# Splitting six PSUM banks four and two between maxima and scores in a 16-head attention

## Chip, cores and metric

One Trainium2 chip, one of its cores. The metric is the device time of one execution in microseconds (us). The kernel before takes 4480.93 us (median of three runs, 4480.48 to 4482.56).

## The reference

Eight sequences of 512 rows and 256 columns go through four layers. Each layer adds an attention and a feed-forward part to `x`. The change lies in the first three attention-like parts, which all have 16 heads of 16 columns: the cross attention of layer 0, the mixture-of-heads attention that is layer 0's feed-forward part, and the cross attention of layer 1. Cut to what matters:

```python
q, k, v = heads(xn @ Wq + bq), heads(ctx @ Wk + bk), heads(ctx @ Wv + bv)   # 16 heads of 16
a = softmax(q @ k.T / sqrt(16))            # 512 x 512 for each head
x = x + merge(a @ v) @ Wo + bo
```

In the mixture part `q` is normalised by head and scaled, and the heads' sum is weighted by gates.

## The kernel before, in words

`softmax_attentions` does the three parts in one phase of 24 rounds: 3 parts by 8 sequences. The phase's exponentials run from 77.3 to 1747.7 us of the trace. A round is written as 32 steps (`STEPS`), and each engine walks the same steps by itself, tied to the others only by semaphores. There is no planner: the order is the tables `TURNS` (line 120) and the step functions.

For every head two products are made of the same operands. The first product, keys on the free axis, is there for its row maximum alone: TensorE writes a 128 x 512 tile `ps_max` (`for_maximum`, line 753), VectorE reduces it to one number for each row (`maximum`, line 482, the instruction at 485). The maxima, negated and split in two, are turned round on TensorE (`negmax` fill, line 827) and copied by ScalarE into eight extra rows of the query stack (`take_negmax`, line 684), so that the second product, keys on partitions, comes out with the maximum taken off: `ps_sc` (`score`, line 738). ScalarE takes its exponential to `probs` (`exponentials`, line 664, the instruction at 671). Every fourth step TensorE multiplies the last eight tiles of `probs` by the values (`values`, line 763, instruction at 774), into `ps_out`. The maxima run 12 steps (`LEAD`) ahead of the scores.

A step on TensorE is: the fills that are due (projections, turns, `negmax`, `raw`, `y`; all go to the one bank `ps_t` and each waits for the previous one to have been taken out), score, maximum, score, maximum, and after every step with remainder 1 of 4 a group of values. In the step behind the values the order is maximum, score, score, maximum (line 865). A round has 64 scores, 64 maxima and 8 groups of values.

PSUM has eight banks of 128 x 512 numbers: three for `ps_max`, three for `ps_sc`, one each for `ps_out` and `ps_t`. Score number `at` goes to bank `at % 3` and waits for exponential `at - 3`; a maximum's product waits in the same way for reduction `at - 3`. TensorE carries out its instructions in the order written, so a wait of either kind holds back all behind it.

VectorE also takes `v`, `raw` (lines 511 and 513), `y` (line 590 in a cross round, 594 in a mixture round) and `gates`, normalises rows, and does the mixture's small gate work (lines 561 to 579). ScalarE also copies `ps_out` after steps 2, 10, 18 and 26 (`take_out`, line 679), and takes `k`, `q`, `xnT`, `hT` (lines 693 to 701) and `negmax`. The rest of the program, five further phases from about 1750 us on, is left alone.

Of the kernel before, what the change touches and what calls it, by code (L numbers as in the profile page):

```python
# [16 lines left out]
F32 = mybir.dt.float32  # L17
# [3 lines left out]
ACT = mybir.ActivationFunctionType  # L21
AX = mybir.AxisListType

P = 128
SEQS = 8
S = 512
# [122 lines left out]
def softmax_attentions(nc, T, G, name, kind):  # L149
# [9 lines left out]
    q_part, k_part = part_terms()  # L159
    ROWS = HD * len(q_part)  # L160
    LEAD = 12
    BANKS = 3
    SLOTS = 6
    PER = 4
    x_sb, ident, identb, own_rows = G["x"], G["ident"], G["identb"], G["own"]
    with Phase(nc, name) as ph:
# [21 lines left out]
        qstack = [ph.sb(f"qstack{b}", [ROWS + 8, HEADS, S], BF16) for b in range(2)]  # L188
        kstack = [ph.sb(f"kstack{b}", [ROWS + 8, HEADS, S], BF16) for b in range(2)]
        vpad = [ph.sb(f"vpad{b}", [P, TILES, HEADS * (HD + 1) + 15], F32) for b in range(2)]  # L190
        maxes = ph.sb("maxes", [P, TILES, HEADS], F32)
        negmax = ph.sb("negmax", [P, 2, TILES, 4, 2], BF16)
        probs = ph.sb("probs", [P, SLOTS, 2, S], F32)
# [23 lines left out]
        gpart = ph.sb("gpart", [P, TILES], F32)  # L217
        ffo = ph.sb("ffo", [P, 2, D], F32)

        ps_max = ph.ps("ps_max", [P, BANKS, S], F32)  # L220
        ps_sc = ph.ps("ps_sc", [P, BANKS, S], F32)
        ps_out = ph.ps("ps_out", [P, S], F32)
        ps_t = ph.ps("ps_t", [P, S], F32)

# [9 lines left out]
        max_ps, max_taken, neg_step, negmax_ready = (ph.sem("max_ps"), ph.sem("max_taken"), ph.sem("neg_step"),  # L234
                                                     ph.sem("negmax_ready"))
        score_ps, probs_ready, probs_used, out_taken = (ph.sem("score_ps"), ph.sem("probs_ready"),
                                                        ph.sem("probs_used"), ph.sem("out_taken"))
# [199 lines left out]
        def _(dve):  # L437
            V = nc.vector
# [43 lines left out]
            def maximum(q, unit):  # L482
                head, t = unit // 4, unit % 4
                dve.wait_ge(max_ps, q.count(64, unit + 1))
                V.tensor_reduce(maxes[:, t, head:head + 1], ps_max[:, q.count(64, unit) % BANKS, :], AX.X,  # L485
                                ALU.max).then_inc(max_taken, 1)

            def negated(q, g):
# [110 lines left out]
            def steps(q):  # L599
# [3 lines left out]
                for n in range(STEPS):  # L603
# [16 lines left out]
                    if own.there:  # L620
                        maximum(own, 2 * (m % STEPS))
                        maximum(own, 2 * (m % STEPS) + 1)
                        if m % 8 == 7:
                            negated(own, (m % STEPS) // 8)
# [28 lines left out]
        def _(act):  # L653
# [10 lines left out]
            def exponentials(q, n):  # L664
                step = q.count(STEPS, n)
                if step >= SLOTS and (step - SLOTS) % PER == 0:
                    act.wait_ge(probs_used, (step - SLOTS) // PER + 1)
                for j in range(2):
                    at = q.count(64, 2 * n + j)
                    act.wait_ge(score_ps, at + 1)  # L670
                    nc.scalar.activation(probs[:, step % SLOTS, j], ps_sc[:, at % BANKS, :], ACT.Exp,  # L671
                                         scale=HD ** -0.5).then_inc(probs_ready, 1)

            def take_out(q, g):
# [61 lines left out]
        def _(pe):  # L736
            weights_here(pe, Item(0))
            def score(q, n, j):

                g, kt, pair = n // 8, n % 8 // 2, n % 2  # L740
                if n % 8 == 0 and j == 0:
                    pe.wait_ge(taken["negmax"], q.count(4, g + 1))
                if not q.later and n == 0 and j == 0:
                    pe.wait_ge(even_own_ready, 1)
                    pe.wait_ge(odd_own_ready, 1)
                at = q.count(64, 2 * n + j)
                if at >= BANKS:
                    pe.wait_ge(probs_ready, at - BANKS + 1)
                head = 4 * g + 2 * pair + j
                nc.tensor.matmul(ps_sc[:, at % BANKS, :], kstack[q.parity][:, head, kt * P:(kt + 1) * P],  # L750
                                 qstack[q.parity][:, head, :], start=True, stop=True).then_inc(score_ps, 1)

            def for_maximum(q, unit):
                head, t = unit // 4, unit % 4
                if unit == 0:
                    pe.wait_ge(stack_in, q.count(192, 192))
                at = q.count(64, unit)
                if at >= BANKS:
                    pe.wait_ge(max_taken, at - BANKS + 1)
                nc.tensor.matmul(ps_max[:, at % BANKS, :], qstack[q.parity][0:ROWS, head, t * P:(t + 1) * P],  # L760
                                 kstack[q.parity][0:ROWS, head, :], start=True, stop=True).then_inc(max_ps, 1)

            def values(q, first, waited):
# [2218 lines left out]
def more_scratch(nc, T):  # L2982
# [4 lines left out]

PHASES = [
    (softmax_attentions, "L0x", ""),
    (quantised_ffn, "L1f", ""),  # L2990
    (feature_attention, "L2x", ""),
# [66 lines left out]
```

## Time and profile before

| | |
|---|---|
| Median of three runs | 4480.93 us |
| The profiled execution: its time, and its span from first to last instruction | 4479.25 us, 4477.1 us |
| TensorE, VectorE, ScalarE, GpSimd busy over the span | 94%, 66%, 57%, 18% |
| The phase, 77.3 to 1747.7 us | 24 rounds |
| A cross round between cross rounds | 68.2 us |
| A mixture round between mixture rounds | 75.3 us |
| The last two rounds | 60.0 and 54.3 us |

Times in the profile are microseconds unless marked ns. TensorE has two rows: PE is the matmuls, PEld the loading of weights, which runs while an earlier matmul is under way. "Idle before" is an engine's idle time just ahead of an instruction, with what ended it. L485 is line 485.

### The profile page before, as it was taken

What the parts mean: (1) busy time and instruction counts of PE and PEld (TensorE: products, weight loads), DVE (VectorE), ACT (ScalarE), POOL (GpSimd) and SP (SyncE); (2) the same over time, 40 slices, a digit from 0 to 9 for tenths busy, and PEclk for the clock granted to TensorE, in tenths of its full rate; (3) what the DMA queues carried; (4) which work ended last, traced back from release to release, by engine and by line L of the source; (5) the groups of instructions that cost most, each with busy time, mean ns of one, the idle gap of its engine ahead of it and who ended that gap; (6) DMA issues with size and microseconds to landing.
All of it is one profiled execution on the core that took longest, in us unless ns stands there. A gap on an engine that the chain in (4) does not pass through costs nothing. (4 is left out here: it accounts for less than half of the span.)

```text
span 4477.1 us, 66439 instructions
## 1 busy us (share of the span) xinstructions
PE 4224.6 (94%) x23716; PEld 2400.0 (54%) x23750; DVE 2965.5 (66%) x7431; ACT 2542.5 (57%) x6408; POOL 811.8 (18%) x576
## 2 busy tenths in 40 slices
PE   6999999999999997888989999999999998999999
PEld 2343344444343342577446666666666665556555
DVE  5767777777777675967765677676676766334333
ACT  3767666666666765743546676767777675111111
POOL 2322444443322311622000000000000000000000
PEclk9999999999999998999999999999999999999999
DMA  8456455445455461000100100110101102000000
GB/s 160 74 78 85 65 66 80 60 64 68 68 75 83 66 83 61 1 20 10 76 12 27 37 30 28 32 32 27 32 27 32 33 26 73 5 5 5 10 5 10
DMA packets 182844, 204.97 MB, mean 46 GB/s; under 512 B 44651, under 2 KB 165099, under 8 KB 180854
## 3 DMA queue, kind: packets, MB, share of 16 engines
q1 hardware_dynamic: 180886, 199.15, 24.3%
q8 instruction: 192, 3.15, 0.3%
q10 hardware_dynamic: 1632, 1.57, 0.3%
q14 instruction: 134, 1.10, 0.1%
HBM read 139.90 MB, written 60.78 MB: 45 GB/s over the span
## 5 line engine op out<-in xcount | busy, mean ns | idle before, releaser
L485 DVE TENSOR_REDUCE L0x_maxes<-L0x_ps_max 128x1 f32<-128x512 f32 x1536 | 976.2, 683 | 288.6 <-PE L0x_ps_max L760 287.0
L671 ACT ACTIVATE L0x_probs<-L0x_ps_sc 128x512 f32<-128x512 f32 x1536 | 822.6, 607 | 360.7 <-PE L0x_ps_sc L750 356.7
L760 PE MATMUL L0x_ps_max<-L0x_kstack,L0x_qstack 96*128 96x512 bf16 x1536 | 587.3, 383 | 22.6 <-DVE L0x_maxes L485 21.3
L2765 ACT ACTIVATE L3x_pexp<-L3x_ps,L3x_nmax 128x77 f32<-128x77 f32 (+2 forms) x1536 | 601.4, 433 | 0.0
L750 PE MATMUL L0x_ps_sc<-L0x_qstack,L0x_kstack 104*128 104x512 bf16 x1536 | 557.0, 383 | 11.5 <-ACT L0x_probs L671 11.0
L2647 DVE TENSOR_REDUCE L3x_nmax<-L3x_ps 128x2 f32<-128x154 f32 (+2 forms) x768 | 346.3, 506 | 242.5 <-PE L3x_ps L2878 240.1
L2773 ACT COPY L3x_pT<-L3x_ps 128x512 f32<-128x512 f32 x512 | 275.1, 593 | 225.8 <-PE L3x_ps L2886 225.4
L2265 ACT ACTIVATE L3f_act_g<-L3f_ps_gu 128x512 f32<-128x512 f32 x128 | 76.4, 597 | 542.4 <-PE L3f_ps_gu L2311 542.3
L774 PE MATMUL L0x_ps_out<-L0x_probs,L0x_vpad 128*32 128x512 f32 x3072 | 369.4, 598 | 1.1 <-ACT L0x_probs L671 1.1
L2663 DVE TENSOR_SCALAR L3x_pexp<-L3x_pexp,L3x_rsum 128x77 f32<-128x77 f32 (+2 forms) x1536 | 357.7, 305 | 6.8
L2765 ACT ACTIVATION_READ_ACCUMULATOR L3x_pexp<-L3x_ps,L3x_nmax 128x1 f32 x1536 | 359.6, 235 | 0.0
L2208 DVE TENSOR_TENSOR L3f_h<-L3f_act_g,L3f_ps_gu 128x512 f32<-128x512 f32 x128 | 88.0, 687 | 383.4 <-ACT L3f_act_g L2265 383.1
L760 PEld LDWEIGHTS L0x_ps_max<-L0x_kstack,L0x_qstack 96*128 96x128 bf16 x1536 | 150.8, 98 | 282.7 <-DVE L0x_maxes L485 168.0
L2904 PE MATMUL L3x_ps<-L3x_pT,L3x_v 128*64 128x128 f32 x4096 | 279.9, 279 | 0.7 <-ACT L3x_oT L2781 0.7
L2886 PEld LDWEIGHTS L3x_ps<-ident,L3x_pexp 128*128 128x128 f32 x2048 | 239.1, 141 | 73.4 <-issue 55.5
L2886 PE MATMUL L3x_ps<-ident,L3x_pexp 128*128 128x128 f32 x2048 | 266.1, 273 | 0.9 <-DVE L3x_pexp L2663 0.9
L750 PEld LDWEIGHTS L0x_ps_sc<-L0x_qstack,L0x_kstack 104*128 104x128 bf16 x1536 | 150.4, 98 | 211.2 <-ACT L0x_probs L671 81.1
L2608 POOL TENSOR_TENSOR L3x_v<-L3x_v,L3x_relv 128x256 f32<-128x256 f32 x32 | 23.4, 731 | 1294.1 <-ACT L3x_v L2748 1294.1
L2311 PE MATMUL L3f_ps_gu<-L3f_xnT,L3f_wg 128*128 128x512 f32 x512 | 243.1, 597 | 1.8 <-DMA L3f_wd<-in_L3f_wd 1.8
L2322 PE MATMUL L3f_ps_y<-L3f_wd,L3f_h 128*128 128x256 f32 x1024 | 242.4, 380 | 1.5 <-DVE x_res L2218 1.5
L2904 PEld LDWEIGHTS L3x_ps<-L3x_pT,L3x_v 128*64 128x64 f32 x4096 | 218.3, 136 | 43.4 <-issue 42.5
L2311 PE MATMUL L3f_ps_gu<-L3f_xnT,L3f_wu 128*128 128x512 f32 x512 | 241.0, 593 | 0.0
(377 smaller groups left out, 6823.5 us busy)
## 6 DMA issues: line engine op xcount, KB each, us to landing
L0x_kstack<-parts_scratch SPq DMA_DIRECT2D x141, 256.0 KB, 10.0
L0x_qstack<-parts_scratch SPq DMA_DIRECT2D x141, 256.0 KB, 14.5
parts_scratch<-L0x_kparts SPq DMA_DIRECT2D x24, 768.0 KB, 3.7
parts_scratch<-L0x_qparts SPq DMA_DIRECT2D x24, 768.0 KB, 5.0
rel_scratch<-L3x_rel_e SPq DMA_DIRECT2D x32, 408.0 KB, 2.4
L3x_rel_d<-prob_scratch SPq DMA_DIRECT2D x32, 408.0 KB, 3.1
L0x_kv_in<-in_ctxT SPq DMA_DIRECT2D x16, 512.0 KB, 4.2
L3x_rel_t<-rel_scratch SPq DMA_DIRECT2D x32, 154.0 KB, 2.3
```

What stands on the lines that cost most here:

```text
L485: V.tensor_reduce(maxes[:, t, head:head + 1], ps_max[:, q.count(64, unit) % BANKS, :], AX.X, ALU.max).then_inc(max_taken, 1)
L671: nc.scalar.activation(probs[:, step % SLOTS, j], ps_sc[:, at % BANKS, :], ACT.Exp, scale=HD ** -0.5).then_inc(probs_ready, 1)
L750: nc.tensor.matmul(ps_sc[:, at % BANKS, :], kstack[q.parity][:, head, kt * P:(kt + 1) * P], qstack[q.parity][:, head, :], start=True, stop ...
L760: nc.tensor.matmul(ps_max[:, at % BANKS, :], qstack[q.parity][0:ROWS, head, t * P:(t + 1) * P], kstack[q.parity][0:ROWS, head, :], start=T ...
L774: i = nc.tensor.matmul(ps_out[32 * j:32 * j + 32, :], vpad[q.parity][:, kt, (HD + 1) * head:(HD + 1) * head + 32], probs[:, q.count(STEPS, ...
L2311: i = nc.tensor.matmul(ps_gu[:, n % 2, k], w[:, ci, n * P:(n + 1) * P], xnT[:, ci, :], start=(ci == 0), stop=(ci == C - 1))
L2647: i = V.tensor_reduce(nmax[:, n % 4, s], ps[:, bank:bank + 2, a:b], AX.X, ALU.max, negate=True)
L2663: i = V.tensor_scalar(pexp[:, m % 4, e, a:b], pexp[:, m % 4, e, a:b], rsum[:, m % 4, s, e:e + 1], None, ALU.mult)
L2765: i = nc.scalar.activation(pexp[:, n % 4, e, a:b], ps[:, SB + 2 * (n % 2) + e, a:b], ACT.Exp, bias=nmax[:, n % 4, s, e:e + 1], accum_out=s ...
L2773: nc.scalar.copy(pT[:, m % 2, e], ps[:, TB + e]).then_inc(pt_ready, 1)
L2886: i = nc.tensor.transpose(ps[:, TB + e, kt * P:(kt + 1) * P], pexp[:, m % 4, e, kt * P:(kt + 1) * P], ident[:])
L2904: i = nc.tensor.matmul(ps[DIMH * e:DIMH * (e + 1), OB, at:at + P], v[g % 2][:, vt, h * DIMH:(h + 1) * DIMH], pT[:, m % 2, e, kt * P:(kt + ...
```

## The change

The one constant `BANKS = 3` becomes two: the maxima get four banks, the scores two. The allocations, the bank numbers and the distances of the two waits follow.

```diff
-    BANKS = 3
+    MAX_BANKS = 4
+    SCORE_BANKS = 2
...
-        ps_max = ph.ps("ps_max", [P, BANKS, S], F32)
-        ps_sc = ph.ps("ps_sc", [P, BANKS, S], F32)
+        ps_max = ph.ps("ps_max", [P, MAX_BANKS, S], F32)
+        ps_sc = ph.ps("ps_sc", [P, SCORE_BANKS, S], F32)
...
-                V.tensor_reduce(maxes[:, t, head:head + 1], ps_max[:, q.count(64, unit) % BANKS, :], AX.X,
+                V.tensor_reduce(maxes[:, t, head:head + 1], ps_max[:, q.count(64, unit) % MAX_BANKS, :], AX.X,
...
-                    nc.scalar.activation(probs[:, step % SLOTS, j], ps_sc[:, at % BANKS, :], ACT.Exp,
+                    nc.scalar.activation(probs[:, step % SLOTS, j], ps_sc[:, at % SCORE_BANKS, :], ACT.Exp,
...
-                if at >= BANKS:
-                    pe.wait_ge(probs_ready, at - BANKS + 1)
+                if at >= SCORE_BANKS:
+                    pe.wait_ge(probs_ready, at - SCORE_BANKS + 1)
...
-                nc.tensor.matmul(ps_sc[:, at % BANKS, :], kstack[q.parity][:, head, kt * P:(kt + 1) * P],
+                nc.tensor.matmul(ps_sc[:, at % SCORE_BANKS, :], kstack[q.parity][:, head, kt * P:(kt + 1) * P],
...
-                if at >= BANKS:
-                    pe.wait_ge(max_taken, at - BANKS + 1)
-                nc.tensor.matmul(ps_max[:, at % BANKS, :], qstack[q.parity][0:ROWS, head, t * P:(t + 1) * P],
+                if at >= MAX_BANKS:
+                    pe.wait_ge(max_taken, at - MAX_BANKS + 1)
+                nc.tensor.matmul(ps_max[:, at % MAX_BANKS, :], qstack[q.parity][0:ROWS, head, t * P:(t + 1) * P],
```

## Rows read from the trace of the kernel before

**Rows 1.** The page, busy time (share of the span) and instructions

```profile
PE 4224.6 (94%) x23716; PEld 2400.0 (54%) x23750; DVE 2965.5 (66%) x7431; ACT 2542.5 (57%) x6408; POOL 811.8 (18%) x576
```

**Rows 2.** Stretches: length; busy of PE, PEld, DVE, ACT, POOL; PEclk; DMA; GB/s

```profile
345.20:413.40 68.20, 66.17 (x354) 27.08 (x352) 48.98 (x98) 47.28 (x82) 19.71 (x12) 1.00 0.54 78
...
1000.40:1075.70 75.30, 70.25 (x386) 32.36 (x384) 58.05 (x122) 47.57 (x82) 34.11 (x15) 0.98 0.47 63
```

**Rows 3.** Waits of PEld in the phase: total us, times, longest

```profile
PEld L0x_ps_max L760 <- DVE L0x_maxes L485: 159.3, 230, 2.8
PEld L0x_ps_sc L750 <- ACT L0x_probs L671: 81.1, 185, 0.9
```

**Rows 4.** The same in one cross round, 413.4 to 481.6 us

```profile
PEld L0x_ps_max L760 <- DVE L0x_maxes L485: 6.0, 9, 0.8
PEld L0x_ps_sc L750 <- ACT L0x_probs L671: 3.4, 8, 0.9
```

**Rows 5.** Timeline of PEld in that round: start, us, [idle before, releaser]

```profile
413.69 0.10 PEld L760 LDWEIGHTS L0x_ps_max<-L0x_kstack,L0x_qstack 96*128 96x128 bf16 x1 [0.53 <-DVE L0x_maxes L485]
...
417.06 0.10 PEld L760 LDWEIGHTS L0x_ps_max<-L0x_kstack,L0x_qstack 96*128 96x128 bf16 x1 [0.84 <-DVE L0x_maxes L485]
...
439.62 0.10 PEld L760 LDWEIGHTS L0x_ps_max<-L0x_kstack,L0x_qstack 96*128 96x128 bf16 x1 [0.51 <-DVE L0x_maxes L485]
...
441.79 0.42 PEld L782 LDWEIGHTS L0x_ps_t<-ident,L0x_xn 128*128 128x128 f32 x4 [0.84 <-ACT L0x_qstack L684]
```

**Rows 6.** Timeline of the last round, where no maxima are left

```profile
1733.60 5.01 ACT L671 ACTIVATE L0x_probs<-L0x_ps_sc 128x512 f32<-128x512 f32 x10
...
1739.36 0.33 PEld L750 LDWEIGHTS L0x_ps_sc<-L0x_qstack,L0x_kstack 104*128 104x128 bf16 x3 [0.84 <-ACT L0x_probs L671]
...
1739.85 1.09 ACT L671 ACTIVATE L0x_probs<-L0x_ps_sc 128x512 f32<-128x512 f32 x2 [1.25 <-PE L0x_ps_sc L750]
1740.50 0.10 PEld L750 LDWEIGHTS L0x_ps_sc<-L0x_qstack,L0x_kstack 104*128 104x128 bf16 x1 [0.81 <-ACT L0x_probs L671]
```

**Rows 7.** The page's group of the exponentials: busy, mean ns of one, idle before

```profile
L671 ACT ACTIVATE L0x_probs<-L0x_ps_sc 128x512 f32<-128x512 f32 x1536 | 822.6, 607 | 360.7 <-PE L0x_ps_sc L750 356.7
```

**Rows 8.** Timeline of the cross round behind 413 us, places that are priced

```profile
417.77 1.08 ACT L671 ACTIVATE L0x_probs<-L0x_ps_sc 128x512 f32<-128x512 f32 x2 [2.24 <-PE L0x_ps_sc L750]
...
417.95 0.38 PE L750 MATMUL L0x_ps_sc<-L0x_qstack,L0x_kstack 104*128 104x512 bf16 x1
...
421.13 0.20 PEld L827 LDWEIGHTS L0x_ps_t<-identb,L0x_negmax 128*8 128x8 bf16 x4 [0.65 <-DVE L0x_htok L513]
...
458.92 1.08 ACT L671 ACTIVATE L0x_probs<-L0x_ps_sc 128x512 f32<-128x512 f32 x2
...
459.87 0.38 PE L750 MATMUL L0x_ps_sc<-L0x_qstack,L0x_kstack 104*128 104x512 bf16 x1
...
467.31 2.05 ACT L671 ACTIVATE L0x_probs<-L0x_ps_sc 128x512 f32<-128x512 f32 x4
...
467.95 0.39 PE L750 MATMUL L0x_ps_sc<-L0x_qstack,L0x_kstack 104*128 104x512 bf16 x1
...
474.37 2.10 ACT L671 ACTIVATE L0x_probs<-L0x_ps_sc 128x512 f32<-128x512 f32 x4
```

**Rows 9.** Timeline of a mixture round at its second `y` fill

```profile
1052.44 1.59 PEld L795 LDWEIGHTS L0x_ps_t<-L0x_wo_mixture,L0x_hT 128*128 128x128 f32 x8 [0.84 <-ACT L0x_qstack L684]
...
1057.04 0.88 DVE L594 SCALAR_TENSOR_TENSOR L0x_ffo<-L0x_ps_t,L0x_gscale,L0x_bo_mixture 128x256 f32<-128x256 f32 x2
...
1058.56 0.10 PEld L760 LDWEIGHTS L0x_ps_max<-L0x_kstack,L0x_qstack 96*128 96x128 bf16 x1 [2.84 <-DVE L0x_maxes L485]
1058.57 2.65 PEld L795 LDWEIGHTS L0x_ps_t<-L0x_wo_mixture,L0x_hT 128*128 128x128 f32 x8
```

**Rows 10.** Stretches there, columns as in rows 2: idle ahead, then that fill

```profile
1055.90:1058.40 2.50, 0.12 (x1) 0.00 (x0) 2.43 (x5) 1.14 (x3) 1.29 (x2) 1.00 0.25 90
1058.50:1061.30 2.80, 2.73 (x8) 2.21 (x9) 1.80 (x4) 0.00 (x0) 2.72 (x3) 0.64 0.54 188
```

## The prediction

> **What bounds the kernel now.** I read the page's busy line first: TensorE is busy 94% of the span, VectorE 66%, ScalarE 57% [rows 1]. Then the stretches cut at the rounds of the phase that the change touches. In a cross round of 68.2 us TensorE is busy 66.17, VectorE 48.98 and ScalarE 47.28 us, and a mixture round of 75.3 us looks alike with 70.25, 58.05 and 47.57 [rows 2]. So TensorE bounds the phase. The other two have room on average, and what they can do is make TensorE wait for a bank. Any such wait that nothing later absorbs is added to the time, because TensorE works through its instructions in order.
>
> Third, the list of waits of the weight loads. In the phase they waited for a reduction 230 times, 159.3 us in all, and for an exponential 185 times, 81.1 us [rows 3]. Read plainly, the maxima wait twice as long, and a fourth bank is for them. The timeline says otherwise. The load behind each group of values shows 0.84 us idle whatever comes there: 0.84 put down to the reduction at 417.06, and 0.84 put down to a copy of ScalarE ahead of a turn at 441.79 [rows 5]. That is the tail of the values' own matmuls, not a bank. In the cross round behind 413.4 us nine waits for a reduction make 6.0 us [rows 4]. Four of them are such tails; five are real, 6.0 less 3.36, or 2.64 us: three in a row before the values at 415.2, of which 413.69 is the first, one before a projection, and that of 0.51 at 439.62 [rows 5]. A load of 0.10 us that follows the last one at 0.22 has 0.12 ahead of it anyway, so the five are worth about 2.05 us of a round. The score side has eight, 3.4 us [rows 4].
>
> **The fourth bank of the maxima.** No instruction is added or taken. The reductions stay as many, 64 a round, and VectorE stays in order. At most the 2.05 us of a cross round go. Not all will: a product that no longer waits for its own bank soon meets a fill, which waits for VectorE or ScalarE to have taken the last one out of the only `ps_t`, or a score.
>
> **The bank that the scores lose.** A score now waits for the exponential two before it. Three numbers decide. Alone, from the score's load to its exponential's start is 0.49 us (1739.36 to 1739.85, [rows 6]); the exponential takes about 0.60 (mean 607 ns, [rows 7]); the next load follows its end by 0.05 (1740.50, [rows 6]). So a bank comes round in 1.14 us, and two banks allow a score every 0.57. ScalarE with a full queue does ten in 5.01, one every 0.50 [rows 6]. TensorE itself can issue a score and a product in 0.44, at 0.22 each. So whenever TensorE has just come from values or a fill, and could run ahead by a third score, it stops. Because a load runs 0.21 us ahead of its matmul, about the first 0.15 us of lateness costs nothing.
>
> I carried this through one cross round, from one group of values to the next, with the durations of the trace. Where a delay meets a fill that waits for VectorE or ScalarE anyway, it vanishes; where it comes right before values, it stays. What stays, in order:
> - Step 3, score matmul at 417.95. Its exponential two before starts at 417.77 and ends 0.6 later, so the score goes at 418.43, 0.48 late. The product of a maximum behind it is late with it, VectorE's reductions end 0.32 later, and the `negmax` fill, which waits for VectorE at 421.13, is 0.32 late [rows 8]: +0.32.
> - The eight steps behind: +0.07, since the fourth bank gives most back at the `v` fill.
> - Before the values at 441: the 0.51 wait at 439.62 goes [rows 5] and a score wait of half its worth comes: -0.17.
> - Before the values at 460: the matmul of 459.87 must wait for the second of the pair that starts at 458.92 and lasts 1.08 [rows 8]: 460.00 and 0.07 make 460.07: +0.20.
> - Behind these values: +0.16.
> - Before the values at 468.5: four exponentials from 467.31 in 2.05 us, late because ScalarE takes `q` first. The score at 467.95 waited for the first; with two banks it waits for the second, one exponential later [rows 8]: +0.49. The whole of a lost bank, right ahead of the values.
> - Steps 27 to 29: four from 474.37 in 2.10, behind the copy of `ps_out` [rows 8]. The third score comes 0.98 late, the maxima with it, the `negmax` fill again waits for the reductions: +0.30.
> - Behind the last values: +0.25 by the next `raw` fill.
> - Steps 0 and 1: the three waits that begin with that of 0.53 [rows 5] go, and scores at the loop's 0.57 take their place: -0.05.
> That is +1.57, and about 0.1 more because I took the loop 0.05 too short in two places: +1.7 us for a cross round. ScalarE's whole list for these rounds stays as long as it was.
>
> A mixture round keeps less. Its fills are longer and absorb more, the same walk leaves +0.24, +0.49, +0.22, +0.29 and +0.20 with -0.05: +1.4. And it holds the one long wait on a reduction, 2.84 us before 1058.56, behind the gates' small operations [rows 9]. With a fourth bank the product goes before them. The second `y` fill then waits only for VectorE's taking of the first, done at 1057.04 plus 0.88, or 1057.92 [rows 9], where the bank came free only with the reduction behind it. That is some 0.6 us, and as the fill's place is then set by VectorE, 0.4 of the delay before it is absorbed. The clock adds to it: after 2.50 us with TensorE busy for 0.12, the granted clock is 0.64 of full over the next 2.8 us [rows 10], so part of it at the 1.2 GHz level, and this fill takes 2.65 us where the first took 1.59 [rows 9]. With products and scores moved into the gap it shrinks to about 1.3 us, and I take the clock to stay: 0.8 of the 1.06 us reach the path. So 1.4 less 1.8: -0.4. Such rounds are five.
>
> **The sum.** Ten plain cross rounds at +1.7: +17. Six rounds at the borders of the parts, which mix the fills of both kinds, at +1.0, between the two: +6. Five mixture rounds: -2. The first round, +2. The last two have few fills between scores. In the last no maxima are left, TensorE stands between loops of exponentials, and three of its eight groups of values come one exponential (0.49) later, with 20 scores at 0.57 in place of 0.50: +3.5, and +2.5 for the one before it. In all +29 us. The phases behind are shifted, not changed. Against the profiled execution, 4479.25 us: 4508. The median of the runs is 1.7 above it, so 4510 by that; I say 4509.
>
> Bounds: from below, all 2.05 us of a cross round's waits on reductions come back and no score costs anything, -49 us over 24 rounds. From above, each of the 192 stretches between values keeps one whole exponential of 0.49 and the maxima give nothing: +94. My sum stands between, since I found a full 0.49 in one of the eight stretches.
>
> **Rivals.** *Faster: the reductions' waits were the dearer ones.* The place is the step before values and before a fill; the price is half to all of the 49 us, 4432 to 4456. It decides if the score's wait stays below the 0.15 us that the early load hides. The Trainium skill ("Perfetto Trace Analysis", Optimization Strategy) has it that the same gap repeating on the engine that should be saturated can mean that PSUM has too few buffers. The gaps repeat here, but the larger part is the values' tail [rows 4, 5], and there are as many real gaps on the side that loses a bank. Chance 0.07.
>
> *No change.* Two banks are enough for an engine that is busy 47.28 of 68.2 us [rows 2], and every delay falls where a fill waits anyway. For it: five of my nine places have a small sum. Against it: two are right ahead of values, where nothing absorbs. 4472 to 4488, chance 0.10.
>
> *Much slower.* Delays pile up over several stretches, or the clock falls more often. One fall costs about the 1.06 us of that fill and as much in what is behind it; once a round it is some 40 us more, 4550. In cross rounds the granted clock is 1.00 [rows 2] with eight score waits, none near 2.5 us. The Trainium skill ("TensorE: Matmul & The Clock Gate", A second HAM failure mode) warns of bank cycling that lets TensorE idle in short pieces until the clock oscillates; the trace does not show it at these lengths. Chance 0.09.
>
> That the change does not do what it says I leave out: eight banks are used before and after, and 64 tiles a round divide by four and by two.
>
> **The numbers.** The forecast, 4490 to 4536, has 0.74; over 4536 0.09; within 0.2% of before (9 us, about what can be told from no change) 0.10; faster 0.07. So slower 0.83. The range is 4486 to 4536.
>
> **What would show it.** In the changed profile: waits on line 750 for line 671 well over 185, and over 81 us; the 0.5 us waits before 413 and 439 gone, the 0.84 ones still there; cross rounds near 69.9 us, mixture rounds near 75 with no fall of the clock, the last near 58; line 485 and line 671 unchanged in busy time. I am wrong if cross rounds are at or below 68.2, or if mixture rounds keep the fall.

## The result, and the profile after

The changed kernel takes 4507.39 us (median of four runs, 4504.70 to 4509.49) against 4480.70 for the kernel before beside it: a ratio of 1.006, 95% interval 1.0048 to 1.0073. It is 27 us slower; the forecast was 4509.

The profiled execution took 4505.59 us, its span is 4503.7, so 26.6 above the span before. That is three things. The phase, from the first to the last exponential group, runs from 71.9 to 1774.7 us, 1702.8 against 1670.4 before: +32.4. It began 5.4 us earlier. What lies behind it takes 2729.0 against 2729.4.

The earlier start has two parts. From the first product for a maximum to the first exponential it is 14.2 us (57.7 to 71.9) where it was 16.4 (60.9 to 77.3). Most of that part belongs to the change: over all profiles of this study the same stretch takes 14.2 to 15.2 us in the five kernels with four banks for the maxima, 16.0 to 17.2 in the seven with three, and 20.0 with two. The forecast had no term for it. The other 3.2 us lie ahead of that first product, whose place varies from 57.6 to 60.9 us between profiles; nothing explains that here. So the length of the phase and of single rounds are the finer measures, and both are used below.

The page's busy line and the stretches (columns as in [rows 2]) of the changed kernel. The four stretches are a cross round, a mixture round, a border round and the last round; then the whole phase.

```profile
PE 4232.0 (94%) x23750; PEld 2361.7 (52%) x23750; DVE 2974.4 (66%) x7431; ACT 2558.2 (57%) x6408; POOL 812.4 (18%) x576
...
346.50:416.30 69.80, 66.76 (x354) 25.95 (x354) 49.34 (x99) 47.96 (x81) 19.71 (x12) 1.00 0.52 76
1008.10:1083.50 75.40, 69.87 (x386) 30.00 (x386) 59.01 (x123) 47.92 (x82) 34.14 (x15) 1.00 0.48 63
631.50:706.70 75.20, 69.62 (x370) 28.35 (x370) 54.00 (x102) 47.78 (x81) 31.62 (x13) 0.98 0.48 64
1717.40:1774.70 57.30, 51.02 (x284) 17.28 (x282) 30.93 (x58) 42.66 (x73) 0.00 (x0) 1.00 0.00 1
71.90:1774.70 1702.80, 1602.08 (x8567) 637.37 (x8567) 1230.15 (x2469) 1143.81 (x1916) 553.84 (x277) 1.00 0.49 69
```

Nothing of the work has changed: the shares of the page are those of [rows 1], and a cross round has VectorE busy for 49.34 us (48.98 before) and ScalarE for 47.96 (47.28). The round is 1.6 us longer all the same (69.8 against 68.2). The time is in waits. Those of the weight loads, in the phase (total us, times, longest) and then in the cross round behind 416.3 us, which answer to [rows 3, 4]:

```profile
PEld L0x_ps_sc L751 <- ACT L0x_probs L672: 276.6, 639, 1.2
PEld L0x_ps_max L761 <- DVE L0x_maxes L486: 65.4, 78, 0.8
...
PEld L0x_ps_sc L751 <- ACT L0x_probs L672: 11.7, 27, 0.9
PEld L0x_ps_max L761 <- DVE L0x_maxes L486: 2.5, 3, 0.8
```

The waits on a reduction fell from 230 to 78. Those 78 are all the values' tail, 0.84 us each, 65.4 in all: no real wait for a bank of the maxima is left. In the kernel before 95 of the 230 were such tails and 135, of 79.7 us together, were real. The waits on an exponential rose from 185 to 639 and from 81.1 to 276.6 us. In the cross round they are 8.3 us more and the round is 1.6 us longer; the real waits on reductions that went make 2.6 of the difference, and the rest lies where TensorE would have waited anyway. The timeline of the weight loads shows two places of that round:

```profile
419.80 0.10 PEld L761 LDWEIGHTS L0x_ps_max<-L0x_kstack,L0x_qstack 96*128 96x128 bf16 x1 [0.84 <-DVE L0x_maxes L486]
...
421.16 0.10 PEld L751 LDWEIGHTS L0x_ps_sc<-L0x_qstack,L0x_kstack 104*128 104x128 bf16 x1 [0.81 <-ACT L0x_probs L672]
...
421.64 0.10 PEld L751 LDWEIGHTS L0x_ps_sc<-L0x_qstack,L0x_kstack 104*128 104x128 bf16 x1 [0.37 <-ACT L0x_probs L672]
...
424.20 0.20 PEld L828 LDWEIGHTS L0x_ps_t<-identb,L0x_negmax 128*8 128x8 bf16 x4 [0.97 <-DVE L0x_htok L514]
...
471.30 0.10 PEld L751 LDWEIGHTS L0x_ps_sc<-L0x_qstack,L0x_kstack 104*128 104x128 bf16 x1 [0.89 <-ACT L0x_probs L672]
...
471.78 0.10 PEld L751 LDWEIGHTS L0x_ps_sc<-L0x_qstack,L0x_kstack 104*128 104x128 bf16 x1 [0.37 <-ACT L0x_probs L672]
...
472.32 0.16 PEld L775 LDWEIGHTS L0x_ps_out<-L0x_probs,L0x_vpad 128*32 128x32 f32 x8 [0.43 <-issue]
```

The first line is the tail of values, the same 0.84 us as in [rows 5], put down to a reduction by chance. The next three lines are the forecast's step 3: scores held at 421.16 and 421.64, the maxima's products behind them late, and the `negmax` fill still waiting for VectorE, with 0.97 us idle ahead where 0.65 stood [rows 8]. The last three are the place with a whole exponential right ahead of values.

Both kernels issue the same loads in the same order, so they can be laid side by side from the first values of the round. By how much more the changed kernel is late at each place, in us:

| Place in the cross round | Measured | Forecast |
|---|---|---|
| Step 3, up to the `negmax` fill | +0.33 | +0.32 |
| The eight steps behind | +0.09 | +0.07 |
| Before the values at 441 | -0.17 | -0.17 |
| Before the values at 460 | +0.20 | +0.20 |
| Behind these values | +0.17 | +0.16 |
| Before the values at 468.5 | +0.49 | +0.49 |
| Steps 27 to 29 | +0.41 | +0.30 |
| Behind the last values, with steps 0 and 1 | +0.05 | +0.20 |
| The round | +1.57 | +1.57, 1.7 with the allowance |

And all rounds, from first exponential to first exponential:

| Rounds | Measured | Forecast |
|---|---|---|
| The first | +2.1 | +2 |
| Ten cross rounds (+1.55 to +1.63 each) | +15.7 | +17 |
| Six border rounds (+0.2, +0.3, +4.0, +0.5, +2.8, +3.1) | +10.9 | +6 |
| Five mixture rounds (-0.2, -1.3, and +0.0 to +0.1 three times) | -1.3 | -2 |
| The last two | +2.1 and +2.9 | +2.5 and +3.5 |
| The phase | +32.4 | +29 |

The -1.3 of one mixture round is a fall of the granted clock in the kernel before that lasted 6.8 us there (from 830.6) and 3.4 in the four others: that round took 76.6 us, those 75.3 to 75.5. And the first round's +2.1 stands against the 2.2 us gained ahead of it: from the first product for a maximum to the round's end it is 79.6 us against 79.7 (80.4 in a second profile of the changed kernel, number 11).

In a mixture round the forecast's long wait is gone and the clock stays up (columns of the timeline as above):

```profile
1060.88 1.59 PEld L796 LDWEIGHTS L0x_ps_t<-L0x_wo_mixture,L0x_hT 128*128 128x128 f32 x8 [0.84 <-ACT L0x_qstack L685]
...
1066.17 1.59 PEld L796 LDWEIGHTS L0x_ps_t<-L0x_wo_mixture,L0x_hT 128*128 128x128 f32 x8 [1.52 <-DVE L0x_ffo L595]
```

The second `y` fill waits for VectorE's taking of the first, 1.52 us where a product stood for 2.84 (TensorE is idle for 1.02 and 2.55 of them, by the matmuls), and takes 1.59 where it took 2.65 [rows 9]; from fill to fill it is 5.29 against 6.13. The stretch with this fill gains 2.1 us. Yet the round is 75.4 us, not shorter than before. What took it back stands at its end, in two rows of VectorE and GpSimd:

```profile
1075.67 1.27 POOL L394 TENSOR_TENSOR x_res<-x_res,L0x_ffo 128x512 f32<-128x512 f32 x1
1075.99 0.99 DVE L493 TENSOR_SCALAR L0x_negmax<-L0x_maxes 128x16 bf16<-128x16 f32 x1
```

The negation of 16 numbers a row, 0.18 us when it runs alone, takes 0.99 and ends 0.04 us behind GpSimd's addition of the output. The `negmax` fill waits for it. The round is shifted enough for these two to meet, as they do in all five mixture rounds: steps 27 to 29 cost +1.1 us where +0.29 was forecast. The border round at 631.5 us has the same thing with a split of the queries:

```profile
696.44 0.18 DVE L493 TENSOR_SCALAR L0x_negmax<-L0x_maxes 128x16 bf16<-128x16 f32 x1
696.64 2.12 POOL L381 TENSOR_TENSOR L0x_qparts<-L0x_qf,L0x_qparts 128x1024 bf16<-128x1024 f32 x1
696.65 2.15 DVE L495 SCALAR_TENSOR_TENSOR L0x_negmax<-L0x_maxes,L0x_negmax 128x16 bf16<-128x16 f32 x1
698.91 0.23 PEld L828 LDWEIGHTS L0x_ps_t<-identb,L0x_negmax 128*8 128x8 bf16 x4 [2.38 <-issue]
```

The weight loads stand for 2.38 us, and the granted clock falls to the 1.2 GHz level for 3.4 us from 700 us on. (In the kernel before the negation was held there too, for 1.26 us at 690.1, and the loads stood for 1.66. In the first two border rounds it went the other way: the negation took 0.89 and 0.90 us at 548.0 and 619.3 before, and is not held with the change, so those rounds grow by 0.2 and 0.3 only.) The changed kernel has such falls at 700, 1195 and 1270 us, the kernel before had one in each mixture round, near 755, 831, 909, 984 and 1059. The falls at 1195 and 1270 follow no long wait: over the 45 us ahead of each, TensorE is busy for 42.86, and no load waited longer than 1.3 us.

### The profile page after: what moved, and what is told of

The parts are those of the page before. It is cut to its first block and busy times, and to the rows that moved or that the text cites. A ratio compares the mean times of both kernels' runs of the same rounds, so it can differ in the third digit from the quotient of the medians.

```text
span 4503.7 us, 66473 instructions
## 1 busy us (share of the span) xinstructions
PE 4232.0 (94%) x23750; PEld 2361.7 (52%) x23750; DVE 2974.4 (66%) x7431; ACT 2558.2 (57%) x6408; POOL 812.4 (18%) x576
## 3 DMA queue, kind: packets, MB, share of 16 engines
q10 hardware_dynamic: 1632, 1.57, 0.3%
## 5 line engine op out<-in xcount | busy, mean ns | idle before, releaser
L672 ACT ACTIVATE L0x_probs<-L0x_ps_sc 128x512 f32<-128x512 f32 x1536 | 838.0, 602 | 360.8 <-PE L0x_ps_sc L751 352.8
L2323 PEld LDWEIGHTS L3f_ps_y<-L3f_wd,L3f_h 128*128 128x128 f32 x1024 | 193.3, 190 | 81.1 <-issue 53.7
```

The source lines that it names most:

```text
L2323: i = nc.tensor.matmul(ps_y[:, n % 2, 0:D], h[:, e % 2, hc, t * P:(t + 1) * P], wd[:, 2 * e + hc, :], start=(hc == 0), stop=(hc == 1))
```

## Experiments

Time in us is the median, with the range of the runs; the ratio is to the kernel before on the same chip (4480.9 to 4481.6 us) with its 95% interval. "Phase" is from the first to the last group of exponentials, 1670.4 before and 1702.8 with the change; it is that of the one profiled execution, which in number 1 is the slowest of its runs and in numbers 7 and 8 the fastest.

**1. The lost bank alone.** Three banks for maxima, two for scores, one bank unused.

```diff
-    MAX_BANKS = 4
+    MAX_BANKS = 3
```

> Three banks for maxima, two for scores, one bank unused: the score side's loss without the maxima's gain. Theory (the lost score bank costs about 1.8 us a cross round, the fourth bank gives 0.2 back there and some 1.2 us and the fall of the clock in a mixture round): cross rounds 70.0 us where the changed kernel has 69.75, mixture rounds 76.5 to 77 with the long wait on a reduction back, 4515 to 4525 us. Rival (the fourth bank is idle, what the changed kernel lost and won in mixture rounds is where clock falls happened to land): cross 69.75, mixture 75.4, 4507 us.

4513.22 (4511.18 to 4517.84), 1.0072 [1.0057, 1.0087]. Stretches of a cross and a mixture round, then the waits in the phase:

```profile
349.40:419.40 70.00, 66.97 (x354) 26.23 (x353) 49.38 (x99) 48.02 (x81) 19.71 (x12) 1.00 0.53 76
1015.30:1092.10 76.80, 71.33 (x386) 31.32 (x385) 58.35 (x123) 48.00 (x81) 34.09 (x15) 0.98 0.45 62
...
PEld L0x_ps_sc L751 <- ACT L0x_probs L672: 276.2, 643, 1.2
PEld L0x_ps_max L761 <- DVE L0x_maxes L486: 81.0, 98, 2.1
```

The waits on exponentials are those of the changed kernel (276.6 us, 639). The bank that the scores lose makes the loss by itself. The fourth bank of the maxima gives back 0.17 us of a cross round, all of it at one place, before the values at 441. In mixture rounds it gives nothing where the clock stays (two of the five take 75.4 us here too) and up to 1.4 where this kernel has a fall, as in the stretch shown, with the clock at 0.98 against 1.00. Over the phase, 1712.4 against 1702.8, it is 9.6 us; by the medians, each less its kernel before (31.7 here, 26.7 and, in number 11, 28.0 for the changed kernel), 4 to 5. The time, 4513, lies between what the theory (4515 or more) and the rival (4507) had. That the bank is worth half or all of the 49 us of waits on reductions is out. Nor are the waits that left the list its doing: of the 79.7 us that were real, 64.1 are gone here already, with three banks (20 waits, 15.6 us, are left beside 78 tails), since TensorE now stops at a score first.

**2. The mirror.** Two banks for maxima, four for scores.

```diff
-    MAX_BANKS = 4
-    SCORE_BANKS = 2
+    MAX_BANKS = 2
+    SCORE_BANKS = 4
```

> The mirror: two banks for maxima, four for scores. Theory (a side with two banks is bound by the way round of one bank, about 0.43 to the start, 0.68 for the reduction and 0.05 to the next product, 1.16 us or 0.58 a tile, and VectorE's own pace is 0.60, so the loss is one reduction ahead of values wherever VectorE is behind, and VectorE has more other work than ScalarE): cross rounds 70 to 72 us, slower than the changed kernel, 4520 to 4560 us. Rival (six banks are six banks, what counts is only that one side has two): as the changed kernel, 4507 within 5 us.

4541.33 (4540.68 to 4542.16), 1.0134 [1.0119, 1.0149]; cross round 70.7, mixture rounds 78.3 to 78.5, phase 1730.2. The wait of the loads in the phase:

```profile
PEld L0x_ps_max L761 <- DVE L0x_maxes L486: 335.3, 667, 3.5
```

Two banks are short for either side. A reduction is longer than an exponential (683 ns against 602 in the page's groups of the changed kernel), which would explain that the maxima miss theirs more; no run separates this from VectorE's other work. Three and three is the best of the three divisions of six.

**3 and 4. Is it the place ahead of values that costs?** The values are moved ahead of the step's second score and its product, once with three and three, once with four and two.

```diff
                     if behind_values and q.there:
                         score(q, n, 0)
+                    if n % PER == 1 and (q if n > 1 else q.plus(-1)).there:
+                        values(q if n > 1 else q.plus(-1), (n - 5) % STEPS, False)
                     if q.there:
                         score(q, n, 1)
...
-                    if n % PER == 1 and (q if n > 1 else q.plus(-1)).there:
-                        values(q if n > 1 else q.plus(-1), (n - 5) % STEPS, q.there)
```

> Kernel before, but the values of a step are computed ahead of the step's second score and maximum. Theory (what is lost is what TensorE waits right ahead of values; with the values put before the last pair, 1.9 us of matmuls lie where it waited, and the banks come free meanwhile): the waits of 0.5 us ahead of the values vanish, 0.5 to 1 us a round less, 4457 to 4470 us. Rival (the waits only move behind the values, because ScalarE and VectorE then start one tile short): 4475 to 4490 us.

> The changed kernel with the values ahead of the step's second score and maximum. Theory (half of the loss of the score bank stood right ahead of values, 0.7 of 1.6 us a round, and is now covered by them): cross rounds near 69.0 or less, 4480 to 4492 us, and the distance to the same order with three and three banks is smaller than 27 us, about 15. Rival (the loss is the slower way round of a score bank wherever it stands): distance to three and three in the same order stays at 27 us or grows.

Three and three: 4497.46 (4496.62 to 4499.12), 1.0037 [1.0024, 1.0049], phase 1691.3. Four and two: 4509.22 (4507.29 to 4513.52), 1.0063 [1.0048, 1.0078], phase 1700.5. A cross round of each, then the waits in the phase of the first:

```profile
347.60:416.40 68.80, 65.46 (x354) 27.44 (x352) 49.13 (x99) 47.87 (x82) 19.72 (x12) 1.00 0.54 77
...
PEld L0x_ps_out L774 <- ACT L0x_probs L671: 38.7, 91, 1.4
```

```profile
347.30:417.00 69.70, 66.77 (x354) 26.13 (x354) 49.34 (x98) 48.66 (x81) 19.75 (x12) 1.00 0.53 76
```

Number 3 missed both its theory (4457 to 4470) and its rival (4475 to 4490): moving the values costs 16 us by itself. The 91 waits for an exponential in the list, 38.7 us, are not the reason. All but two of them are 0.43 or 0.23 us long, and the kernel before has the same idle time ahead of its values, 0.43 us in 142 and 0.23 in 48 of the 192 groups, put down there to "issue"; the score just ahead waits for the same exponential. What makes the move dear stays open. From number 3 to two banks for scores it is 0.8 or 0.9 us a cross round and 12 us in all, not 1.57 and 27. So the price of the lost bank depends on where the values stand, but this pair does not say which place it is.

**5 and 6. Place by place.** Three and three banks, but the wait of a score is put as near as two banks would force it: in number 5 only at the last score ahead of values, in number 6 at all others.

```diff
-                if at >= BANKS:
-                    pe.wait_ge(probs_ready, at - BANKS + 1)
+                apart = 2 if n % PER == 1 and j == 1 else BANKS
+                if at >= apart:
+                    pe.wait_ge(probs_ready, at - apart + 1)
```

(In number 6 the 2 and `BANKS` change places.)

> Three banks each as before, but the last score ahead of every group of values (8 of 64 a round) waits for the exponential two before it, not three. Theory (what is lost right ahead of values stays, +0.20 and +0.49 of my walk): a cross round of 68.2 grows to 68.9, the phase by some 14 us, 4493 to 4498 us. Rival (the loss goes by the number of scores that wait, one in eight): +0.2 a round, about 4485 us.

> Three banks each as before; every score but the last ahead of values waits for the exponential two before it. Theory (my walk without the two places ahead of values, and without the fourth bank's gain: 0.32 + 0.07 + 0.16 + 0.30 + 0.25 = 1.1): cross rounds 69.3 us, the phase +22 us; the excess of this run and of the one with the near wait ahead of values alone add up to that of three and two banks, 1.7 us a cross round. Rival (by number of scores, seven in eight): 69.7 us, and the sum falls short of additive where one delay hides the other.

Number 5: 4494.15 (4493.66 to 4496.91), 1.0031 [1.0019, 1.0043], phase 1687.5. Number 6: 4507.74 (4506.28 to 4509.46), 1.0061 [1.0047, 1.0075], phase 1701.5. For each a cross round and the waits of the scores in the phase:

```profile
348.60:417.60 69.00, 66.51 (x354) 27.02 (x352) 49.15 (x98) 47.43 (x82) 19.73 (x12) 1.00 0.53 77
...
PEld L0x_ps_sc L751 <- ACT L0x_probs L671: 115.7, 233, 0.9
```

```profile
348.30:418.10 69.80, 66.72 (x353) 26.40 (x352) 49.27 (x98) 47.92 (x80) 19.67 (x11) 1.00 0.52 76
...
PEld L0x_ps_sc L751 <- ACT L0x_probs L671: 241.2, 548, 1.2
```

The near wait alone, with every bank in place, gives such losses: it is the distance of the wait, not the number of banks. One wait in eight, ahead of values, makes 0.8 us of a cross round and 13 of the time. The other seven make 1.6 and 27. The two do not add: 0.8 and 1.6 are 2.4, and all waits together, as number 1 has them, make 1.8 in that stretch (70.0 less 68.2). Place by place, laid beside the kernel before as above (the 0.16 and the 0.49 as one):

| Up to | Step 3 | Eight steps | 441 | 460 | 468.5 | Steps 27 to 29 | Next round |
|---|---|---|---|---|---|---|---|
| Number 5 | 0.00 | 0.00 | 0.00 | +0.20 | +0.49 | +0.08 | 0.00 |
| Number 6 | +0.33 | +0.09 | 0.00 | +0.15 | +0.65 | +0.41 | +0.01 |
| Number 1 | +0.33 | +0.09 | 0.00 | +0.20 | +0.66 | +0.42 | +0.06 |

Number 5 has the two terms of the walk ahead of values, 0.20 and 0.49, to the hundredth. But number 6 has them nearly whole as well, though its scores right ahead of values keep the far wait: the first score of the same step is held instead (0.89 us at 473.28), and the delay reaches the values all the same. So "right ahead of values" is dear, but taking the near wait away from there alone saves little (1.64 us a round for 1.77).

**7 and 8. The small operations beside GpSimd.** In mixture rounds GpSimd's split of the keys is held until the gates' small operations are through, with three and three banks (7) and with four and two (8).

```diff
+                    if ahead.later and after_k == 1 and q.plus(-1).there and not q.plus(-1).cross and not ahead.cross:
+                        pool.wait_ge(gate_step, q.plus(-1).own(15, 15))
                     if ahead.later and after_k in (0, 1):
```

> Kernel before, but in the five mixture rounds GpSimd starts the second half of the keys' split only when VectorE's gate operations are done. In the trace three small VectorE operations there (0.56, 1.75 and 1.97 us for a few elements) each end within 0.04 us of the end of a GpSimd operation. Theory (GpSimd holds them up, they make the 2.84 us wait on a reduction and the fall of the clock behind it): they drop to 0.2 us, the long wait goes, mixture rounds 75.3 to 76.6 become 71.5 to 73, the whole 12 to 20 us less, 4461 to 4469 us. Rival (the operations are slow by themselves, or TensorE waits for the fill's bank anyway): mixture rounds within 0.5 us of before, 4480 us.

> The changed kernel with the same hold on GpSimd. Theory (in mixture rounds the fourth bank's gain was that it passed the long wait and kept the clock, which hid a loss of 1.4 us on the score side; with the long wait gone there is nothing for it to pass): mixture rounds 1 to 1.5 us above those of three and three banks with the hold, where without it they were even (75.4 against 75.3), and the distance between the two kernels grows from 27 to 32 to 38 us. Rival (the fourth bank gives as much everywhere): the distance stays 27 us.

Number 7: 4485.07 (4479.51 to 4488.35, eleven runs), 1.0009 [1.0, 1.0018]. Number 8: 4508.28 (4499.99 to 4510.31), 1.0059 [1.0047, 1.0072]; mixture round 74.9, where number 7 has 75.6 to 77.0, phase 1696.6. The timeline of the kernel before at the gates of a mixture round, which the forecast did not look at:

```profile
1052.68 1.90 POOL L378 TENSOR_TENSOR L0x_kparts<-L0x_kf,one 128x1024 bf16<-128x1024 f32 x1
1052.85 1.75 DVE L574 SCALAR_TENSOR_TENSOR L0x_gpart<-L0x_gshare,L0x_gsw 128x4 f32<-128x4 f32 x1
...
1054.66 2.12 POOL L380 TENSOR_TENSOR L0x_kparts<-L0x_kf,L0x_kparts 128x1024 bf16<-128x1024 f32 x1
1054.83 1.97 DVE L577 SCALAR_TENSOR_TENSOR L0x_gtop<-L0x_gsw,L0x_gshare 128x4 f32<-128x4 f32 x1
```

And of number 7:

```profile
1053.74 0.16 DVE L576 SCALAR_TENSOR_TENSOR L0x_gpart<-L0x_gshare,L0x_gsw 128x4 f32<-128x4 f32 x1
1054.13 0.16 DVE L579 SCALAR_TENSOR_TENSOR L0x_gtop<-L0x_gsw,L0x_gshare 128x4 f32<-128x4 f32 x1
...
1066.01 2.12 POOL L380 TENSOR_TENSOR L0x_qparts<-L0x_qf,L0x_qparts 128x1024 bf16<-128x1024 f32 x1
1067.17 1.00 DVE L494 TENSOR_SCALAR L0x_negmax<-L0x_maxes 128x16 bf16<-128x16 f32 x1
1068.21 1.19 DVE L496 SCALAR_TENSOR_TENSOR L0x_negmax<-L0x_maxes,L0x_negmax 128x16 bf16<-128x16 f32 x1
1069.51 0.23 PEld L829 LDWEIGHTS L0x_ps_t<-identb,L0x_negmax 128*8 128x8 bf16 x4 [2.40 <-issue]
```

Four numbers a row took 1.75 and 1.97 us beside GpSimd and take 0.16 without it. That was the long wait of [rows 9]: VectorE had been standing in these operations, not working. But number 7 gains nothing. The held GpSimd work comes later and meets the negation, the loads stand for 2.40 us there in place of 2.84 at the `y` fill, and the clock falls in each mixture round as before, only later (near 766, 841, 916, 995 and 1070 us). So its theory of 12 to 20 us less failed; the rival had the number, 4480, but not the reason, since the operations are not slow by themselves. For number 8 the theory failed too: it had the distance of the two divisions grow to 32 to 38 us, and it is 23. In number 8 the loads stand for 1.91 us at the negation, and no fall follows in the mixture rounds.

Number 8 also prices one fall. In the round from 1154 us on it has none, the changed kernel has that at 1195, and the two go alike but for the stretch with the fall, which is 1.62 us longer (round 73.0 against 74.6 us).

**9 and 10. Both meetings taken away.** GpSimd also waits for the negation of the next round's first maxima ahead of the second half of the queries' split, and, where a cross round is ahead, holds the first half of the keys' split too, with three and three (9) and four and two (10).

```diff
+                    hold_at = 0 if ahead.cross else 1
+                    if ahead.later and after_k == hold_at and q.plus(-1).there and not q.plus(-1).cross:
+                        pool.wait_ge(gate_step, q.plus(-1).own(15, 15))
+                    if ahead.later and after_q == 2 and not ahead.cross:
+                        pool.wait_ge(negmax_ready, q.plus(1).count(4, 1))
                     if ahead.later and after_k in (0, 1):
```

> Three banks each, with two holds on GpSimd: no second half of a keys' split before the gates are done (for a cross round ahead, no first half either), and no second half of a queries' split before the next round's first maxima are negated. In the run with the first hold alone the gates' operations fell to 0.16 us, but GpSimd's later operations then held up the negation (1.00 us at 1067.2) with a wait of 2.4 us ahead of the turned maxima, and the clock fell there. Theory (the hold-up only moved): with both, no VectorE operation of a few elements takes over 0.6 us, mixture rounds 72 to 73 us, the clock keeps, 4462 to 4472 us. Rival (something else sets the mixture rounds, or the fills of the stacks now come late): 75 us and 4480 us or more.

> The changed split of banks, four and two, with the same two holds. Theory (without the long waits the fourth bank has nothing to pass in mixture rounds, the score side costs there what it does in cross rounds): mixture rounds 1 to 1.5 us above the run of three and three with both holds, cross rounds 69.7 against 68.2 as ever, distance of the two 30 to 36 us. Rival (the fourth bank still pays in mixture rounds): mixture rounds even, distance 22 us or less.

Number 9: 4464.40 (4459.39 to 4467.32), 0.9962 [0.9949, 0.9976], faster than both kernels. Number 10: 4496.51 (4495.02 to 4497.97), 1.0037 [1.0024, 1.0050]. A mixture round and the phase of each:

```profile
986.20:1058.50 72.30, 68.83 (x386) 31.46 (x384) 54.70 (x122) 47.50 (x82) 34.10 (x15) 1.00 0.50 66
...
76.60:1733.50 1656.90, 1585.43 (x8567) 668.58 (x8565) 1198.17 (x2468) 1128.19 (x1916) 552.38 (x277) 1.00 0.51 71
```

```profile
999.50:1073.00 73.50, 69.60 (x386) 30.10 (x386) 54.98 (x123) 47.95 (x82) 34.11 (x15) 1.00 0.49 65
...
74.90:1765.80 1690.90, 1600.72 (x8567) 637.22 (x8566) 1205.04 (x2469) 1143.92 (x1916) 553.42 (x277) 1.00 0.50 70
```

With the two meetings gone (an operation on eight elements is still held, to 0.56 us, five times) a mixture round is 72.3 us and VectorE's busy time in the phase falls from 1220.35 us before to 1198.17 with the same 2468 instructions. The five falls of the clock in mixture rounds are gone; two stand elsewhere, at 103 us in the first round (65.9 us for 63.3) and at 1243. And here the two divisions stand 32.1 us apart, 34.0 by the phase: four and two costs +1.5 us in a cross round (69.7 against 68.2) and +1.1 or 1.2 in a mixture round, and steps 27 to 29 of a mixture round cost +0.33, where the forecast had +0.29 and the changed kernel +1.1. The six border rounds together make +5.8, where the forecast had 6. This comes near the change's price with the other effect out of the way; what is left in it is falls at different places, one of them in number 10's last round, which takes 59.8 us for 57.3. In the kernels as given the mixture rounds cost nothing and the border rounds more, which together comes near the same: 32.4 us of the phase.

**11. The changed kernel again**, unchanged, as to whether its falls of the clock are there each time.

> The changed kernel once more, for a second profile of it beside the others on one chip. If its falls of the clock belong to the order of the work, they stand again at 700, 1195 and 1270 us, and rounds 9, 16 and 17 (of 24) take 75.2, 74.6 and 75.5 us again; if they are chance, they stand elsewhere and those rounds take about 72. Cross rounds 69.7 either way; 4503 to 4511 us.

4508.85 (4505.86 to 4509.28), 1.0062 [1.0050, 1.0075], phase 1703.4. Two of its border rounds:

```profile
632.50:707.70 75.20, 69.61 (x369) 28.35 (x368) 53.93 (x101) 47.79 (x80) 31.61 (x13) 0.98 0.46 64
1232.90:1308.40 75.50, 70.58 (x370) 28.29 (x370) 53.01 (x120) 48.19 (x82) 22.17 (x14) 0.98 0.48 70
```

The same rounds are long by the same amount, and the clock falls at 701, 1196 and 1271 us again. Those three belong to the order of the work, not to one execution. A fourth, at 766, stands in this profile alone; its round takes 76.0 us for 75.3.

## Why the prediction was right, and where its terms were not

- **What bounds the phase, and which waits are real.** Right. The 0.84 us behind values is in every kernel, whoever it is put down to. Of 79.7 us of real waits for reductions none is left, and the fourth bank gave back 4 to 10 us (number 1).
- **Two banks allow a score every 0.57 us.** The mechanism is right: numbers 5 and 6 get losses from that distance alone, with no bank taken. The 0.57 itself was not measured by a run of its own.
- **The walk of a cross round.** Right: +1.57 us measured for +1.57 walked, and within 0.02 at the first six places. "Steps 27 to 29: +0.30" was 0.41, and "Behind the last values: +0.25" with "-0.05" was 0.05; that the two misses cancel is luck in part. The "about 0.1 more" was not there; over ten rounds that is 1.3 us.
- **"The whole of a lost bank, right ahead of the values."** The 0.49 us was there. As a reason for the total it was too narrow: the seven waits in eight that stand elsewhere make 1.6 of the 1.8 us by themselves (number 6).
- **Mixture rounds, "1.4 less 1.8: -0.4".** The mechanism came, 2.84 us to 1.52 (the forecast had about 1.3) and the clock stayed; the gain of 1.8 measured 2.1 up to that place. The size of the round did not: +0.1 at 1008 us and -1.3 over the five, all of it from one long fall in the kernel before. The term that failed is +0.29 for steps 27 to 29, which measured +1.1, because the negation took 0.99 us beside GpSimd; with both holds in, where it takes 0.18, the same term is +0.33 (number 10 beside 9). The forecast priced VectorE's queue by the alone times of its operations.
- **"Six rounds at the borders of the parts ... at +1.0": +6.** It was +10.9. Three of them have +0.2 to +0.5 and three +2.8 to +4.0. In the third the cause is seen: 2.15 us of a negation beside GpSimd, 2.38 us of standing loads, and a fall of the clock. The other two have a fall as well, at 1195 and 1270 us, at 1.6 us each; with both holds, which take the meetings away and move the falls, the six make +5.8.
- **The last two rounds.** +2.1 and +2.9 against +2.5 and +3.5. The terms given for the last, three exponentials at 0.49 and 20 scores at 0.07 more, make 2.9 and not 3.5.
- **The sum.** +32.4 in the phase against +29, and 27 in the time, because the phase began 5.4 us earlier, 2.2 of it on the way to the first exponential, which the fourth bank shortens, and 3.2 ahead of that, which no run explains. That the median fell 2 us from the forecast is in part luck: the border rounds were 5 us too low, the start was left out, and the two go against each other.
- **Rivals.** *Faster* is out by the result, and its price for the fourth bank by number 1. *No change* is out by the interval; its ground, an engine busy 47 of 68 us, says nothing of two waits in a row. *Much slower*: the clock fell less often, not more: three times for five between 100 and 1750 us. The Trainium skill ("TensorE: Matmul & The Clock Gate", A second HAM failure mode) has cycling through banks as such a danger; here 639 short waits, 1.2 us at most, left the granted clock at 1.00 in the cross rounds, and the falls whose cause was seen followed single waits of 2.4 to 2.8 us. The falls at 1195 and 1270 had only short waits ahead of them. The kernel before has none in those rounds. Of the kernels with the near wait at most or all of the scores, the changed one and numbers 1, 6, 8 and 11 have one or two there, numbers 4 and 10 none; number 9, with the far wait, has one at 1243. So the page's danger may be at work in those rounds, and no run decides it.

Open: what makes the place of the first product vary by 3 us; what leads to the falls at 1195 and 1270 us; why moving the values costs 16 us.

## What to carry over

Between two uses of a bank the wait's distance sets the pace: work out load, start, work and release of the consumer, divide by the banks, and compare it with the pace of a full queue; then walk one round and see which delays meet a wait that is there anyway. Waits put down to one side by total are no measure of what a bank is worth there: the list had 159 us of them, 80 were real, 64 of these went without any bank being added, and the bank gave 4 to 10. And before a long wait is met with a buffer, look at what the waited-for engine was doing: here it was held by another one, and moving that one's work gave 16 us where the bank cost 27.

## What was not expected of the hardware

Some small VectorE operations on SBUF that start while a GpSimd operation of 1.3 to 2.1 us runs do not end before it does. At 1052.85 us four elements a row take 1.75 us and end 0.02 us behind GpSimd's; at 1054.83 1.97 us, again 0.02 behind; the same instructions take 0.16 us with GpSimd standing (number 7). Others keep their length. Inside one GpSimd operation of the kernel before:

```profile
1050.46 2.14 POOL L375 TENSOR_TENSOR L0x_kf<-L0x_kf,L0x_kparts 128x1024 f32<-128x1024 f32 x1
1050.66 0.17 DVE L567 TENSOR_REDUCE L0x_gtop<-L0x_gtop 128x4 f32<-128x12 f32 x1
```

In the phase of the kernel before all 18 small operations with two inputs in SBUF that start at least 0.3 us before GpSimd is through are held, and so are three negations, which have one input; they end 0.02 to 0.04 us behind GpSimd. All 39 reductions, MAX8 operations and reciprocals with one input in SBUF take their 0.12 to 0.21 us. Over the phase VectorE is 22 us less busy with both holds in, 1198.17 (number 9) against 1220.35 in the kernel before, with the same 2468 instructions:

```profile
77.30:1747.70 1670.40, 1589.66 (x8567) 672.82 (x8565) 1220.35 (x2468) 1128.32 (x1916) 552.48 (x277) 0.99 0.50 71
```

The reductions that read PSUM are not lengthened: a pair at 695.12 takes 1.29 us inside GpSimd's 1.90 from 694.67, and 1.28 at 1077.11 with GpSimd through:

```profile
694.67 1.90 POOL L379 TENSOR_TENSOR L0x_qparts<-L0x_qf,one 128x1024 bf16<-128x1024 f32 x1
695.12 1.29 DVE L486 TENSOR_REDUCE L0x_maxes<-L0x_ps_max 128x1 f32<-128x512 f32 x2 [0.23 <-PE L0x_ps_max L761]
...
1077.11 1.28 DVE L486 TENSOR_REDUCE L0x_maxes<-L0x_ps_max 128x1 f32<-128x512 f32 x2
```

The Trainium skill ("SBUF — State Buffer", SBUF: two separate sides) says that VectorE and GpSimd share one pair of SBUF ports, which whoever starts first keeps for the whole of its instruction, and that a VectorE operation asks for it when it runs in a two-port mode or, beside a GpSimd operation that reads SBUF, when it has two inputs in SBUF. The rows agree for two inputs (the gate operations, the second negation) and for which one waits, and the 39 with one input that keep their length do not speak against it; that the first negation, with one input, runs in a two-port mode no run here shows, only that it was held as well.
